# The reciprocal of the softmax sums in an attention stage: three ScalarE activations replaced by one VectorE reciprocal

## What is computed

```python
x = x + layernorm(attention(layernorm(x)))     # x: (8, 2048, 4096), 32 query heads, 8 kv heads, D = 128
x = x + layernorm(ffn(layernorm(x)))           # a sign-weight FFN with routed scales

# inside attention, after q, k, v and the rotary embedding
scores = einsum('bqhgd,bkhd->bhgqk', qg, k) * scale     # masked above the diagonal
probs  = softmax(scores, axis=-1)
out    = einsum('bhgqk,bkhd->bqhgd', probs, v)
out    = einsum('bse,fe->bsf', out, w_out)
```

## Time and profile before

| | |
|---|---|
| runs shown, median of 2 | 9800.63 us (9580.7 and 10020.56) |
| profiled execution | 9392.72 us |
| span of its slowest core | 9391.2 us (all cores 9369.9 to 9391.2) |
| granted TensorE clock, mean | 0.681 of 2.4 GHz |
| TensorE matmul busy | 6268.8 us, 67% of the span |
| ScalarE busy | 1987.7 us, 21% |
| VectorE busy | 1394.5 us, 15% |

### The profile page before, as it was taken

The page is one execution under the profiler, slowest core; times in us unless marked ns, Lnnn a source line. Parts: engine busy times, 40 slices in busy tenths (PEclk is TensorE's granted clock), DMA queues, the critical chain, the costliest instruction groups (busy, mean ns, idle before and its releaser), DMA issues.

```text
span 9391.2 us, 67305 instructions; the slowest of 8 cores (9369.9 to 9391.2 us)
## 1 busy us (share of the span) xinstructions
PE 6268.8 (67%) x22088; PEld 2165.6 (23%) x22496; DVE 1394.5 (15%) x1412; ACT 1987.7 (21%) x3313; POOL 248.0 (3%) x283
## 2 busy tenths in 40 slices
PE   1277777778567888888888886888810077888400
PEld 1133333333111111111111112333400023333100
DVE  3311111111100000000000000000044440000244
ACT  2200000000454443333333330000022211111111
POOL 0011111110000000000000000000000000000000
PEclk6588888889555555555555557999955568999655
DMA  2212221222100000000000003222122212111233
GB/s 87 78 35 40 41 41 34 41 46 73 42 11 25 7 14 15 5 5 5 4 4 4 4 4 103 51 52 52 32 111 112 112 52 50 45 40 46 87 134 143
DMA packets 118325, 443.03 MB, mean 47 GB/s; under 512 B 13665, under 2 KB 87521, under 8 KB 88033
## 3 DMA queue, kind: packets, MB, share of 16 engines
q0 software_dynamic: 16912, 119.74, 7.0%
q10 hardware_dynamic: 12962, 176.18, 4.9%
q1 hardware_dynamic: 88128, 142.78, 4.2%
HBM read 415.78 MB, written 142.61 MB: 59 GB/s over the span
## 4 chain that ended last, share of the span: by engine, by line
PE 65%; DMA 13%; ACT 8%; DVE 8%; issue 4%; another core or an unknown queue 1%; POOL 1%; ACTq 0%; DVEq 0%; POOLq 0%; SPq 0%
PE PA L544 6%; PE PB L358 5%; PE PA L358 5%; DMA wq_sb<-wqkv 4%; PE PB L572 4%; PE PB L859 3%; PE PB L562 3%; PE PA L859 3%; PE PB L697 3%; PE PE L537 3%; PE PA L697 3%; PE PF L537 3%; DVE stats L228 3%; DMA x_t<-xin 3%; PE PA L614 3%
## 5 line engine op out<-in xcount | busy, mean ns | idle before, releaser
L544 PE MATMUL PA<-ptb,ones_bf 128*1 128x512 bf16 (+3 forms) x1280 | 665.7, 520 | 18.7 <-issue 15.9
L358 PE MATMUL PB<-arena,wq_sb 128*128 128x512 bf16 x2006 | 467.8, 393 | 127.4 <-DMA wq_sb<-wqkv 124.9
L358 PE MATMUL PA<-arena,wq_sb 128*128 128x512 bf16 x2006 | 466.4, 392 | 113.0 <-DMA wq_sb<-wqkv 110.6
L594 ACT ACTIVATE ptb<-PB 128x512 bf16<-128x512 f32 (+1 forms) x640 | 333.6, 573 | 625.6 <-PE PB L572 614.3
L614 PE MATMUL PA<-recT_sb,ones_f 1*128 1x512 f32 x256 | 261.2, 1122 | 290.2 <-ACT recT_sb L611 290.2
L572 PE MATMUL PB<-nmxT_sb,ones_bf 1*128 1x512 bf16 (+1 forms) x640 | 371.9, 581 | 25.6 <-PE PA L501 21.3
L859 PE MATMUL PB<-wslot,arena 128*128 128x512 bf16 x1317 | 300.1, 384 | 71.3 <-ACT wslot L829 69.5
L697 PE MATMUL PB<-wslot,arena 128*128 128x512 bf16 x1318 | 298.8, 385 | 61.7 <-DMA wslot<-wout 60.3
L537 PE MATMUL PE<-ptb,vtm 128*128 128x512 bf16 (+3 forms) x624 | 337.6, 541 | 0.0
L562 PE MATMUL PB<-q_sb,k_sb 128*128 128x512 bf16 (+1 forms) x574 | 332.7, 580 | 0.8
L537 PE MATMUL PF<-ptb,vtm 128*128 128x512 bf16 (+3 forms) x616 | 332.8, 540 | 0.0
(11 more groups left out here) (194 smaller groups left out, 6614.3 us busy)
## 6 DMA issues: line engine op xcount, KB each, us to landing
x_t<-xin ACTq DMA_DIRECT2D x32, 2048.0 KB, 9.2
wq_sb<-wqkv POOLq DMA_DIRECT2D x48, 1024.0 KB, 9.3
wslot<-wout POOLq DMA_DIRECT2D x32, 1024.0 KB, 17.0
x2s<-ln2tmp SPq DMA_DIRECT2D x16, 2048.0 KB, 6.3
wslot<-wffn POOLq DMA_DIRECT2D x32, 1024.0 KB, 16.4
x_t<-x2s ACTq DMA_DIRECT2D x16, 2048.0 KB
out<-y_t SPq DMA_DIRECT2D x16, 2048.0 KB, 9.8
Qs<-qout_sb SPq DMA_DIRECT2D x128, 128.0 KB, 7.3
```

Of the source, the lines that this page charges most:

```text
L358: do("tensor", lambda e, p=p, ec=ec, tb=tb, a=sl["ap"]: e.matmul(a[:, :], wq_sb[p][:, ec * 128:(ec + 1) * 128], arena[:, ec * S + tb * 512 ...
L544: e.matmul(sums_ap[0:1, j0 * 128: j0 * 128 + cw], ones_bf1[:, 0:1], ptb[pb][:, j0 * 128: j0 * 128 + cw], start=(kc == 0), stop=(kc == nkc ...
L594: e.activation(ptb[pb][:, j0 * 128: j0 * 128 + cw], a[:, j0 * 128: j0 * 128 + cw], AF.Exp, bias=0.0, scale=1.0),
```

## The change

The three ScalarE instructions that compute Exp(-Ln(s)) are taken out. In their place VectorE runs one `reciprocal` that reads the sums in PSUM (1 partition x 512, f32) and writes the same tile `recT_sb`. The spreading matmul waits for VectorE's count in place of ScalarE's. Nothing else differs.

```diff
-        a1 = do("scalar", lambda e, sp=sp: e.activation(
-            recT_sb[sp][0:1, :], sums_ap[0:1, 0:512], AF.Ln, bias=0.0, scale=1.0),
-            inc="sA", waits=(("sT", pe_grp),))
-        a2 = do("scalar", lambda e, sp=sp: e.mul(
-            recT_sb[sp][0:1, :], recT_sb[sp][0:1, :], -1.0), inc="sA",
-            waits=(("sA", a1),))
-        a3 = do("scalar", lambda e, sp=sp: e.activation(
-            recT_sb[sp][0:1, :], recT_sb[sp][0:1, :], AF.Exp, bias=0.0, scale=1.0),
-            inc="sA", waits=(("sA", a2),))
+        vrc = do("vector", lambda e, sp=sp: e.reciprocal(
+            recT_sb[sp][0:1, :], sums_ap[0:1, 0:512]), inc="sV",
+            waits=(("sT", pe_grp),))
         do("tensor", lambda e, sp=sp: e.matmul(
             sums_ap[:, 0:512], ones_f[:, :], recT_sb[sp][0:1, :],
-            start=True, stop=True), inc="sT", waits=(("sA", a3),))
+            start=True, stop=True), inc="sT", waits=(("sV", vrc),))
```

## The result

Against the kernel before the changed kernel takes 1.0221 of its time, with an interval of 1.0148 to 1.0294. The medians are 9660.24 us (11 executions) and 9577.13 us (10 executions). So it is slower, by an amount that the interval puts on either side of 2%. The lowest executions are 9572.13 and 9394.27 us. The ratio compares only executions in which no die ran at a clearly lower granted clock than the other, so it is not the ratio of the medians, which is 1.0087. That length hardly varies: in the changed kernel's trace it is 3412.4 to 3412.9 us on the eight cores.

A forecast was written before the change was run, and what follows sets the result against it. TensorE sets attention's pace and stands still 2.27 us a group before the spreading matmul; 9392.72 us plus 128 x (3.25 - 2.03) = +156 us gives 9549 us, 1.7% more. Range 9220 to 9900 us.

The forecast's parts named there:

- The path: In attention, TensorE's 2.27 us pause before each of 128 spreading matmuls is on the path; its change moves each group's end equally.
- The hand-overs: Around the reciprocal, PE to DVE 0.10 us and DVE to PE 0.14 us, so the pause becomes D + 0.24 us.
- D: Time of one VectorE reciprocal of 512 elements in attention: 3.25 us forecast, between 0.69 and 5.80; break-even 2.03 us.
- half the 10 ns excess: One-element reciprocal L783 takes 10 ns more than tensor_scalar L230; 5 ns was charged at every element, giving 3.25 us.
- The estimate from the repeat count of 8: Skill's iterative divide read as eight cycles an element: 4.27 us plus some 0.15 us start, time near 9699 us.
- plain mode of one result a cycle: The skill's same section, applied to the reciprocal as to everything else, would give 9222 us.
- The forecast time: Whole kernel: 9392.72 us profiled execution plus 128 x (3.25 - 2.03) = +156 us, 9549 us, 1.7% more.
- The rivals: Four alternatives to the forecast case: slower divide, pipelined division, covered pause, and clock; chances 0.32, 0.18, 0.04 and 0.02.
- Rival 1: Slower divide at the reciprocal, 7.5 ns excess an element, 4.52 us each; loss of 319 us, 9712 us; chance 0.32.
- rival 2: Pipelined division, the 10 ns paid once, reciprocal 0.70 us, pause 0.94 us; 9222 us, 1.8% less; chance 0.18.
- Rival 3: The pause before the spreading matmul is covered, for instance before L501, so nothing moves: 9393 us; chance 0.04.
- Rival 4: A shorter pause lets attention's granted clock rise from 0.50, shrinking stretches by hundreds of us; chance 0.02.

The follow-up runs named there:

- r_twice: Changed kernel with the reciprocal executed twice in a row, the second waiting for the first; attention stage 3851.4 us against 3413.0, lowest execution 10199.86 us.
- r_fold: Kernel before with the product by -1 folded into the Exp's scale, two activations for three; stage 92.0 us shorter, one execution 9302.59 us.
- r_lnfirst: Kernel before with only Ln ahead of the spreading matmul, Exp replacing the copy into bcast_sb; stage 181.8 us shorter, ratio 0.9822.
- r_sizes: Changed kernel plus 28 reciprocals of 14 shapes ahead of the first stage; 3341 to 3358 ns at 512 elements, 6.25 ns for each element.
- r_best_ln: Kernel before with Ln ahead of spreading, Exp behind, tail behind next group's first score chunks, square and column sum moved mid-group; stage 464.0 us shorter, ratio 0.9631.
- r_defer_recip: Changed kernel with the spreading matmul and its followers behind the next group's first two score chunks; stage 356.0 us shorter than before, lowest execution 9053.65 us.
- r_best_recip: Changed kernel with the tail behind the next group's first score chunks, square and column sum moved mid-group; stage 2983.8 us against 3243.7 before, lowest execution 9211.23 us.

## Why the prediction was right or wrong

**The path.** Right. All 128 pauses ahead of the spreading matmul were released by the reciprocal, everything behind it kept its distance (L501 idle 198.4 against 201.9 us), and the stage grew by the pause, within 2 us. r_twice, r_fold and r_lnfirst each gave what "128 times the change of the chain" says, within 3 us.

**The hand-overs.** 0.24 us were taken from the earlier trace rows; 3.60 - 3.346 = 0.25 us were measured.

**The price of the reciprocal.** D was put at 3.25 us and is 3.346 us; the term was 156 us and is 128 x 1.33 = 170 us. The choice of half the 10 ns excess came close, but its reasons were thin, and much of that was luck. By r_sizes the division costs 5.2 ns an element over the 1.04 of an ordinary op. The rest of the 10 ns is a fixed part. On one partition a reciprocal of one element takes 151 ns and the tensor_scalar 142; on 128 both take 12 to 13 ns more. So a single-element row bounded the price from both sides but could not fix it: with the ends that it allowed, the change could be -170 or +483 us.

**What was cited for it.** The estimate from the repeat count of 8 in the Trainium skill's "VectorE: DVE Perf Modes" (walkthrough of the 8-slice pipeline) was 4.42 us; read as eight cycles an element it is too high, as the measured 6.25 ns are six cycles by the 0.96 GHz of that page, an estimate. The same section's plain mode of one result a cycle for everything does not hold for this op either.

**The forecast time.** This is the step that failed. The sum 9392.72 + 156 = 9549 us took a single profiled execution as its base. Both runs shown with it lay higher (9580.7 and 10020.56 us), and over ten executions of the kernel before the median is 9577.13 us and the lowest 9394.27. So the base lay 184 us under the median, more than the whole change, and 9549 us came out 28 us below the median of the kernel that it was said to be slower than: as a time it named a gain where the runs show a loss. The other term, D, was short by only 14 us. The base matches the lowest executions, and beside the lowest of the changed kernel, 9572.13 us, the sum is 23 us low. The text said that the ratio was the better statement, and by the ratio it would have been 1.017 against a measured 1.0221 (1.0148 to 1.0294); it still gave the sum as the forecast. Scaling the median would not have hit either: 1.017 x 9577.13 = 9740 us against the median 9660.24. The two medians are 83 us apart where attention alone grew by 169, so medians of ten and eleven executions do not carry a difference of this size.

**The rivals.** Rival 1 (D near 4.5 us) and rival 2 (D = 0.70) are excluded by the 3.346 us. Rival 3, that the pause was covered, is excluded by r_lnfirst and r_twice. Rival 4, the clock: with pauses of 0.83, 2.27, 3.60 and 7.05 us the granted clock in attention stayed at 0.50 and the length followed the pauses, so a pause of this size, longer or shorter, does not set the level. The chances put 0.49 on within 2% and 0.42 on slower by more; with an interval from 1.5 to 2.9% the measurement itself does not decide between these.

## What to carry to other kernels

Before one op replaces three, look up or measure its time for each element, not for one instruction: here a row of 512 reciprocals costs 3.35 us and three activations with their gaps 2.03. A chain on another engine that an in-order matmul engine waits for should first be shortened or moved behind the next piece's matmuls: r_lnfirst took 182 us and r_best_ln 464 us out of a stage to which this change added 169. A wait taken out can give more than its idle time, since the matmuls on either side overlap again. Once the wait is covered, the choice of the engine goes by what else stands in its list. And a forecast that is small against the spread of executions should be given as a ratio or as a stage's length, not as one execution plus a difference.

## What was not expected of the hardware

- VectorE's reciprocal takes 141 ns plus 6.25 ns an element per partition, from 8 to 1024 elements, and at 512 elements the same within 17 ns from SBUF or PSUM, in f32 or bf16, on 1 or 128 partitions.
- Matmuls in a row overlap, so the spreading pair adds 1.70 us between others and 2.04 between two waits.
- In attention the granted clock stays at 0.50 of 2.4 GHz, 1.2 GHz, also where matmuls follow each other for 32 us and TensorE is busy 436 of 500 us. The QKV stretch of the same program has 0.89. Nothing here says why.
- In r_defer_recip, r_best_recip and r_best_ln the mean level in attention is 0.51 or 0.52 on some cores, and single passes of the spreading matmul take as little as 662 ns in the first and 587 on core 4 of the other two, where the other kernels have 1052 or more. In r_best_ln core 4 has the shorter stage too, 2757.0 us against 2779.7 on core 0, whose shortest pass takes 1056 ns. The source line in r_defer_recip:

```profile
L613 PE MATMUL PA<-recT_sb,ones_f x256: 662/1056/1189, 2457.5 to 5345.6; 1*128 1x512 f32 x128
```
